# Order in a mixing stage's first and last steps: shared products ahead of bias products, page bookkeeping behind the norm, small loads split, two additions a tile

## What is computed

```python
attn_out = ctx @ o_w + o_b + xn
an = _rmsnorm(attn_out, gamma2)
shared = gelu(an @ sh_w1 + sh_b1) @ sh_w2 + sh_b2
logits = an @ router_w + router_b
aff = softmax(logits)
topv, topi = top_k(aff, 3)                       # 31 experts
gates = sum(one_hot(topi, 31) * topv)
routed = sum_e gates_e * (gelu(an @ re_w1_e + re_b1_e) @ re_w2_e) + gates @ re_b2
return shared + routed + an + attn_out           # plus the residual x
```

## Time and profile before

| | us |
|---|---|
| median of 3 runs | 1021.67 (1016.75 to 1024.92) |
| the profiled execution, its own time | 1016.59 |
| its span, first to last instruction | 1014.9 |
| mixing stage within it | about 700 to 849 |
| expert stage | 849 to 1015 |

### The profile page before, as it was taken

One profiled execution on the slowest core, in us unless ns is written; L12 is line 12 of the kernel. 1 busy time (PEld: TensorE's weight loads), 2 busy tenths in 40 slices (PEclk: granted clock), 3 DMA queues, 4 the chain that ended last, 5 costly groups with the idle time before them and its releaser, 6 DMA issues. The chain is left out here.

```text
span 1014.9 us, 18998 instructions
## 1 busy us (share of the span) xinstructions
PE 926.5 (91%) x5504; PEld 689.4 (68%) x5504; DVE 654.6 (64%) x1983; ACT 546.5 (54%) x1370; POOL 451.9 (45%) x584
## 2 busy tenths in 40 slices
PE   7979999996999999959999899999799789999997
PEld 4655555664766666747776676766678546999996
DVE  5966686782696979858777677772366632334555
ACT  5657888784342424447876677763122222555553
POOL 6013574544877887922123222250556440003652
PEclk9979999998999999969999999999899766999999
DMA  7657646433668677889778777763959421445775
GB/s 245 215 179 222 179 127 169 129 97 106 232 231 306 232 283 260 320 255 240 195 192 201 219 199 191 194 195 79 273 190 373 152 99 54 135 133 169 230 229 173
DMA packets 151702, 200.48 MB, mean 198 GB/s; under 512 B 21914, under 2 KB 94393, under 8 KB 151602
## 3 DMA queue, kind: packets, MB, share of 16 engines
q1 hardware_dynamic: 140674, 179.00, 58.1%
q0 software_dynamic: 4608, 12.59, 4.1%
q10 hardware_dynamic: 6320, 7.69, 2.6%
HBM read 121.37 MB, written 77.73 MB: 196 GB/s over the span
## 5 line engine op out<-in xcount | busy, mean ns | idle before, releaser
L1004 DVE CUSTOM_DVE_ANT_0 a_sm<-a_sc,keep_mask_qk 128x512 f32<-128x512 f32 (+3 forms) x256 | 118.4, 482 | 68.8 <-PE a_sc L918 59.9
L716 DVE CUSTOM_DVE_ANT_0 rope_x<-a_sc,keep_mask_qk 128x512 bf16<-128x512 f32 (+3 forms) x256 | 112.1, 486 | 51.3 <-PE a_sc L611 48.3
L992 ACT ACTIVATE a_probs<-a_sm,a_neg 128x512 f32<-128x512 f32 (+3 forms) x256 | 140.1, 552 | 4.0 <-DVE a_neg L1004 3.9
L1318 POOL TENSOR_TENSOR rope_rot<-rope_wqkv 128x512 f32<-128x512 f32 x64 | 93.2, 1473 | 30.8 <-DVE rope_wqkv L1384 30.5
L923 PE MATMUL a_tp<-keep_ident,a_probs 128*128 128x128 f32 x640 | 104.4, 280 | 0.0
L2029 POOL DMA_INDIRECT ex_three<-ks,keep_slots x48 | 48.2, 1005 | 118.7 <-SPq L2053 96.2
L923 PEld LDWEIGHTS a_tp<-keep_ident,a_probs 128*128 128x128 f32 x640 | 74.7, 141 | 25.6 <-issue 17.4
L897 POOL CAST a_ka<-a_ka 64x512 fp32r<-64x512 f32 x48 | 29.2, 609 | 130.8 <-DMA a_qa<-qs 130.2
L1256 PE MATMUL p_ub<-rope_km,rope_wh 128*128 128x512 f32 x256 | 82.0, 402 | 6.0 <-DVE rope_km L1374 6.0
L2139 DVE COPY ex_w<-keep_w 128x514 f32 x78 | 33.5, 430 | 81.7 <-ACT ex_hid L2101 79.3
L2078 PE MATMUL ex_hb<-ex_xT,ex_w 128*128 128x128 f32 x624 | 84.2, 279 | 0.7 <-DVE ex_xT L2141 0.7
(11 more groups left out here) (297 smaller groups left out, 2144.9 us busy)
## 6 DMA issues: line engine op xcount, KB each, us to landing
a_qa<-qs SPq DMA_DIRECT2D x96, 128.0 KB, 3.9
ks<-rope_rot SPq DMA_DIRECT2D x40, 256.0 KB, 3.3
qs<-rope_rot SPq DMA_DIRECT2D x40, 256.0 KB, 2.5
keep_ring<-qs SPq DMA_DIRECT2D x78, 128.0 KB, 2.5
ks<-ex_ysb SPq DMA_DIRECT2D x78, 128.0 KB, 2.2
rope_qm<-qs SPq DMA_DIRECT2D x64, 128.0 KB
rope_km<-ks SPq DMA_DIRECT2D x64, 128.0 KB
qs<-rope_qm SPq DMA_DIRECT2D x32, 256.0 KB, 2.6
```

The lines of the kernel that those rows point to most:

```text
L716: return dve.tensor_tensor_reduce(out=junk[:, JUNK[qb]:JUNK[qb] + n], in0=src, in1=c.mask_qk[:, S - n:S], scale=1.0, scalar=-3e38, op0=ALU ...
L992: act.activation(probs[:, h % PR, rows(qb)], sm[:, h % SM, rows(qb)], ACT.Exp, bias=neg[:, h % 2, qb:qb + 1], scale=-1.0, accum_out=sums[: ...
L1004: return dve.tensor_tensor_reduce(out=sm[:, h % SM, rows(qb)], in0=src[:, 0:n], in1=c.mask_qk[:, S - n:S], scale=-1.0, scalar=3e38, op0=AL ...
L1318: pool.tensor_tensor(rot[:, u % ROT, half, :], prod[:, u % 2, 2 * half, :], prod[:, u % 2, 2 * half + 1, :], op)\
```

## The change

It reorders and splits; only flags of accumulation and where some values stand in PSUM go with it.

1. Small loads: `ob` is issued first on a semaphore of its own (`ob_in`), for which alone POOL's first `bias` waits. `small_in` counts seven: `g2`, `sb2`, `rb`, `sb1`, `rw`, `sw1`, `sw2`. `x1` of step 0 and then `b2` (`b2_in`) are issued by ACT behind `pre(0)`. DVE's `base(0)` moves behind `norm(0)`.
2. `place` is cut in two. Its second half, `settle(b-1)`, stands behind `norm(b)` and ahead of `shared(b-1)`.
3. Behind `hidden(3, 1)` PE does the row product for the table of experts (now into `tp[1]`), then `shared(3)`, then the gates' turns and bias products; the last step's bias products (`last_bias`) come at the very end. `turn_gate` alternates between `tp[0]` and `tp[1]`. DVE copies the table ahead of its bias additions.
4. In `experts`, the additions of step 2 go two to a round, so 12 are left behind the loop instead of 14. Tiles 8 to 11 are stored in the loop; 12 and 13 by ACT and 14 and 15 by POOL at the end.

```diff
         shift_b, end_b, new_b = (tp[1][:, 256 + 32 * i:256 + 32 * i + E] for i in range(3))
-        row_b = tp[0]
+        row_b = tp[1]
         bias_bank = (op[0], op[1], hp[0], hp[1], op[0], op[1])
...
         tile_of, rowed, tables_known = (a.sem(n) for n in ("tile_of", "rowed", "tables_known"))
-        small_in, factors_in, last_scaled = (a.sem(n) for n in ("small_in", "factors_in", "last_scaled"))
+        small_in, ob_in, b2_in, factors_in, last_scaled = (a.sem(n) for n in ("small_in", "ob_in", "b2_in", "factors_in", "last_scaled"))
         x1_in = [a.sem(f"x1_in{i}") for i in range(B)]
...
         block = a.stack.enter_context(nc.Block())
-        NSMALL = 9
+        NSMALL = 7
         LAST = B * H // 2 - 4
...
         def _(act):
+            act.dma_start(ob[:, :], t["L0_ffn_o_b"].to_broadcast([P, D])).then_inc(ob_in, 16)
+            for dst, name in ((g2, "L0_ffn_gamma2"), (sb2, "L0_ffn_sh_b2"), (rb, "L0_ffn_router_b")):
+                act.dma_start(dst[:, :], t[name].to_broadcast([P, dst.shape[1]])).then_inc(small_in, 16)
+            act.dma_start(sb1[:, :], t["L0_ffn_sh_b1"]).then_inc(small_in, 16)
             for dst, name, pat in ((rw, "L0_ffn_router_w", "(k p) n -> p k n"),
...
                 act.dma_start(dst[:, :, :], t[name].rearrange(pat, p=P)).then_inc(small_in, 16)
-            for dst, name in ((ob, "L0_ffn_o_b"), (g2, "L0_ffn_gamma2"), (sb2, "L0_ffn_sh_b2"), (rb, "L0_ffn_router_b")):
-                act.dma_start(dst[:, :], t[name].to_broadcast([P, dst.shape[1]])).then_inc(small_in, 16)
-            act.dma_start(sb1[:, :], t["L0_ffn_sh_b1"]).then_inc(small_in, 16)
-            act.dma_start(b2[:, :], t["L0_ffn_re_b2"]).then_inc(small_in, 16)
...
+            pre(0)
             load_x1(0)
-            pre(0)
+            act.dma_start(b2[:, :], t["L0_ffn_re_b2"]).then_inc(b2_in, 16)
             for b in range(B - 1):
...
                     act.wait_ge(bias_mul, b - 1)
-                act.activation(gateT[:, b % 2, :], tp[0][0:E, :], ACT.Copy).then_inc(g_copied, 1)
+                act.activation(gateT[:, b % 2, :], tp[b % 2][0:E, :], ACT.Copy).then_inc(g_copied, 1)
             for j in range(2):
...
-            def shared(b, more=False):
+            def shared(b):
...
                             mm = pe.matmul(yp[j][:, D * (i % 2):D * (i % 2) + D], hid[:, m, P * i:P * i + P], sw2[:, m, :],
-                                           start=(m == 0), stop=(m == FF // P - 1 and not more))
-                        if more:
-                            mm = pe.matmul(yp[j][:, D * (i % 2):D * (i % 2) + D], gateT[:, b % 2, P * i:P * i + P], b2[:, :],
-                                           start=False, stop=True)
+                                           start=(m == 0 and i % 2 == 0), stop=(b < B - 1 and m == FF // P - 1 and i % 2 == 1))
+                    if b < B - 1:
+                        mm.then_inc(y_mul, 1)
+
+            def last_bias():
+
+                pe.wait_ge(g_copied, B)
+                for j in range(2):
+                    for i in (2 * j, 2 * j + 1):
+                        mm = pe.matmul(yp[j][:, D * (i % 2):D * (i % 2) + D], gateT[:, (B - 1) % 2, P * i:P * i + P], b2[:, :],
+                                       start=False, stop=(i % 2 == 1))
                     mm.then_inc(y_mul, 1)
...
-                if b:
-                    pe.wait_ge(g_copied, b)
+                if b >= 2:
+                    pe.wait_ge(g_copied, b - 1)
+                elif b == 1:
+                    pe.wait_ge(tables_known, 1)
                 for i in range(SB):
-                    mm = pe.transpose(tp[0][0:E, P * i:P * i + P], gate[:, SB * b + i, :], c.ident[:, :])
+                    mm = pe.transpose(tp[b % 2][0:E, P * i:P * i + P], gate[:, SB * b + i, :], c.ident[:, :])
                 mm.then_inc(g_turned, 1)
...
             hidden(B - 1, 1)
+            pe.wait_ge(tile_of, 1)
+            pe.wait_ge(place_read, B)
+            pe.matmul(row_b[0:1, 0:P], of_tile[:, :], c.ident[:, :], start=True, stop=True).then_inc(rowed, 1)
+            shared(B - 1)
+            pe.wait_ge(b2_in, 16)
             pe.wait_ge(gate_ready, 1)
...
             bias(2)
-            pe.wait_ge(g_copied, B)
-            shared(B - 1, more=True)
-            pe.wait_ge(tile_of, 1)
-            pe.matmul(row_b[0:1, 0:P], of_tile[:, :], c.ident[:, :], start=True, stop=True).then_inc(rowed, 1)
+            last_bias()
...
                 if b == 0:
-                    pool.wait_ge(small_in, 16 * NSMALL)
+                    pool.wait_ge(ob_in, 16)
                 pool.wait_ge(xn_in[b % 2], 16 * (b // 2 + 1))
...
                 dve.tensor_copy(c.slots[:, :, cols], pos[:, :, cols]).then_inc(slots_ready, 1)
+
+            def settle(b):
...
             for b in range(B):
-                base(b)
+                if b:
+                    base(b)
                 outputs(b)
...
                 if b:
+                    settle(b - 1)
                     shared(b - 1)
+                else:
+                    base(b)
                 more_base(b)
...
             place(B - 1)
+            settle(B - 1)
...
+            dve.wait_ge(rowed, 1)
+            dve.tensor_copy(c.experts[:, 0:NT], row_b[0:1, 0:NT]).then_inc(tables_known, 1)
             for b in range(B - 1):
...
                     dve.tensor_add(tiles, tiles, bias_bank[j][:, :]).then_inc(bias_added, 1)
-            dve.wait_ge(rowed, 1)
-            dve.tensor_copy(c.experts[:, 0:NT], row_b[0:1, 0:NT]).then_inc(tables_known, 1)
             dve.wait_ge(tick_s, gates_k)
...
             "turned", "x_copied", "w_copied", "h_mul", "h_done", "y_mul", "y_copied", "ye_done"))
-        tick_s, summed, out_s = a.sem("tick"), a.sem("summed"), a.sem("out")
+        tick_s, summed, out_s, out_p = (a.sem(n) for n in ("tick", "summed", "out", "out_p"))
         block = a.stack.enter_context(nc.Block())
...
             return TOPK * SB * (q // SB) + SB * k + q % SB + 1
+
+        added = [MOST[n // (TOPK * SB)] + 2 + (n % (TOPK * SB)) // (1 if n < 2 * TOPK * SB else 2) for n in range((B - 1) * TOPK * SB)]
+
+        def store_out(eng, q, done):
+            eng.wait_ge(summed, adds(q, TOPK - 1))
+            eng.dma_start(out[q // SB, P * (q % SB):P * (q % SB) + P, :], c.base[:, q, :]).then_inc(done, 16)
...
                             .then_inc(three_in[q % SUMS][k], 16)
-
-        def store_out(eng, q):
-            eng.wait_ge(summed, adds(q, TOPK - 1))
-            eng.dma_start(out[q // SB, P * (q % SB):P * (q % SB) + P, :], c.base[:, q, :]).then_inc(out_s, 16)
+            for q in range(TILES - 2, TILES):
+                store_out(pool, q, out_p)
...
                     sp.nop(nofuse=True).then_inc(ye_done, 1)
-                for b in range(B - 2):
-                    q = n - (MOST[b] + 2 + TOPK * SB)
-                    if SB * b <= q + SB * b < SB * b + SB:
-                        store_out(sp, q + SB * b)
-            for q in range(SB * (B - 2), SB * (B - 1)):
-                store_out(sp, q)
-            sp.wait_ge(out_s, 16 * TILES)
+                for b in range(B - 1):
+                    q = n - (added[TOPK * SB * (b + 1) - 1] + 1)
+                    if 0 <= q < SB:
+                        store_out(sp, SB * b + q, out_s)
+            sp.wait_ge(out_p, 16 * 2)
+            sp.wait_ge(out_s, 16 * (TILES - 2))
...
                     act.activation(ysb[:, n % YR, :], yb[n % 2][:, 0:D], ACT.Copy).then_inc(y_copied, 1)
-            for q in range(SB * (B - 1), TILES):
-                store_out(act, q)
+            for q in range(SB * (B - 1), TILES - 2):
+                store_out(act, q, out_s)
...
             ADDS = TOPK * TILES
-            first_round = {r: n for b in range(B - 1) for n in range(SB * TOPK * b, SB * TOPK * (b + 1))
-                           for r in [MOST[b] + 2 + n - SB * TOPK * b] if r < NT}
-
             dve.wait_ge(c.w1_in, 16 * c.w1_loads)
...
                     last_part(r)
-                if r in first_round:
-                    add(first_round[r])
-            for n in range(len(first_round), ADDS):
+                for n, round_ in enumerate(added):
+                    if round_ == r:
+                        add(n)
+            for n in range(len(added), ADDS):
                 add(n)
```

## The result

| | kernel before | kernel after |
|---|---|---|
| device time, median of 4 runs | 1021.71 us (1016.75 to 1024.92) | 1008.38 us (1005.39 to 1009.71) |
| ratio to before | 1 | 0.987 [0.982, 0.992] |
| profiled execution: time, span | 1016.59, 1014.9 us | 1009.71, 1007.8 us |

The change makes the kernel 13.3 us faster by the medians. Beside the first experiments the changed kernel ran once more, on another chip: 1009.06 against 1019.54 us, 0.9906 [0.9885, 0.9927].

The account below looks back on a forecast made before the run. PE, busy 91% of the span, was taken as the bound, with gains where it idles or runs slow. Front 4.7 + tail 13.5 + end 1.0 = 19.2 us; 997.4 from the profiled execution, 1002.5 from the median, taken 999.5, range 990 to 1010.

Parts of the forecast that it names:

- a clock that stays low through the tail: Rival, end of mixing stage: clock stays low, tail gains only 6.4 us, 1004.5 us in all; chance 0.14.
- the front: Start of the mixing stage: 3.9 + 3.1 − 2.3 = 4.7 us gained, bounds 0 and 7.
- The wait for small loads and the clock behind it: Mixing stage's front: PE restarts 3.9 us earlier, and the stretch at half speed behind it saves 3.1 us.
- `x1(0)` late: Front: x1(0), issued later, lands after 8.5 us and holds up DVE; 2.3 us given back, bounds 0 and 4.
- Pages settled: Step 3 of the mixing stage: bookkeeping behind the norm lets PE start 1.8 us earlier, counted inside the 13.5.
- The tail: End of mixing stage: shared products ahead of bias products start the expert stage 13.5 us earlier, bounds 6.4 and 14.9.
- Two additions a tile, and the stores: End of expert stage: additions 1.2 us earlier, last stores partly over POOL; 1.0 us gained, bounds −1 and 1.7.
- front wait changes its owner: Rival, front: small loads or x1 land later and the clock drops anyway; front gains 0, 1002.1 us, chance 0.14.

Follow-up runs that it names:

- Experiment 2: Changed kernel with the load of x1(0) issued ahead of the first norm again; 998.40 us, 0.9795 of the kernel before.
- experiment 7: Changed kernel with the page bookkeeping of steps 0 to 2 back ahead of the norm; 1008.51 us, 0.9881 of the kernel before.
- experiment 8: Changed kernel with the last two output tiles stored from ACT's queue, not GpSimd's; 1006.00 us, 0.9856 of the kernel before.
- both again (9): Changed kernel with x1(0) ahead of the first norm and the last stores from ACT, second run; 996.35 us, 0.9763 of the kernel before.
- GpSimd aside (10): Changed kernel, x1(0) first, last stores from ACT, GpSimd's factor products held until step 0's membership is written; second run 996.16 us, 0.9776.
- experiment 4: Kernel before with only load_x1(0) moved behind pre(0) and base(0) behind the norm; 1019.25 us, 1.0014 of the kernel before.
- experiment 6: Changed kernel with step 3's shared products back behind the bias products of steps 0 to 2; 1013.58 us, 0.9938 of the kernel before.
- experiments 5: Kernel before with the order of the last step alone changed as in the change; 1006.38 us, 0.9857 of the kernel before.

## Why the prediction was right, and where it was not

The whole time, 1008.4 us, lies inside the range of 990 to 1010 and 9 us above the forecast. That it lies inside is luck in part. The forecast's own range was 993 to 1004, and the time is outside it. The wide range reached 1010 for another rival, a clock that stays low through the tail; that did not happen, and the loss that did, in the front, fell outside its own bounds and happened to fit in. Term by term:

- **The wait for small loads and the clock behind it (3.9 + 3.1).** Right. Idle 1.44 us for the 1.7 foreseen, granted clock 1.00 behind it, 7.17 us for 32 products. Experiment 2 measures it free of the rest: 6.0 us for 7.0.
- **`x1(0)` late (−2.3).** This term failed. Two sizes were off and one thing was missing. The landing: 8.5 us assumed, 10.96 and 10.4 measured, at and just above my upper end (10.6). Those rows were the nearer ones for the size, but not the same case throughout: the load with 10.6, `x1(0)` of the kernel before (issued at 705.52, landed at 716.13), had no weights ahead of it, only the small loads and `xn`; the one with 10.2 did stand behind SP's weights. What it held up: the logit addition came 4.5 us after PE's products were through, where I had 2.3 (2.1 by the prediction's own times, 729.3 less 727.2). Missing: when PE idled again (6.27 us), the clock fell again. I had priced this fall as a gain where it vanished and at nothing where a new wait could bring it back. It costs 1.8 us in the first eight products alone. The term is −7.2 (front of after less front of experiment 2), outside my bounds of 0 to −4.
- **GpSimd beside DVE (no term).** The factors landed later too, since all that SP issues went out later, and so GpSimd's products, which before had begun at 728.20 and been over by 732.8, ran through DVE's choice. I had said of `xn(2)` and the next `x1` what their lateness does, and of the factors nothing. What this cost by itself no run separates.
- **Pages settled (1.8, in the tail).** The wait is as worked out: 3.87 us, released by DVE's `keep_bounds`, 1.74 us less. Its value in the stage is 1.1 us (experiment 7).
- **The tail (13.5).** Right in size (14.2) and in mechanism: L1649 directly behind L1764 at clock 1.00, PE's wait for the gates gone. I had reckoned with either PE or SP as what ends the stage, and taken SP. In the kernel after it is PE, whose clock falls at the second bias group; with PE fast it is SP. The two bounds lie within 1 us of each other, which is why the forecast was good in spite of the wrong owner. The rival of a low clock through the tail is out. (By the prediction's own terms its end at the high clock is 829.1 and not 828.9; nothing hangs on it.)
- **Two additions a tile, and the stores (1.0).** The additions: 1.4 us earlier, for 1.2. In the loop they are hidden, as foreseen: four of the six rounds with two additions take the 1.98 us of all others, and the remaining two make it up between them (2.33, then 1.63). The stores: −1.6 for −0.2. I had compared landings (3.1 for 2.1) and not asked what else ends an execution behind a store of GpSimd's queue. The sentence of the Trainium skill (DMA: Bandwidth & Descriptors, Latency and other measured facts) that puts the software path behind the hardware path in its first byte pointed the right way; the trace has 2.8 us to landing for GpSimd's two stores and 2.1 for ACT's, but experiment 8 shows about three times that difference, 2.0 us, at the end.
- **The sum.** 19.2 foreseen, 12.9 measured in the trace: front −1.2 for 4.7, tail 14.2 for 13.5, end −0.1 for 1.0. 1021.7 − 12.9 = 1008.8, the median is 1008.4. Of the 9 us by which the forecast missed, 6 come from the sum and 3 from my taking a value between the profiled execution and the median. The 5 us between those two look like scatter in other stages: this stage started at 695.3 to 705.7 in the traces of unchanged code above it. If so, nothing of it was the change's to win, and the median was the right base; there is only one trace of the kernel before to judge by.
- The rival "front wait changes its owner" (1002.1, chance 0.14) had the mechanism, with 4.7 as its largest loss. It was 5.9.

## What to carry to other kernels

Here a load that was moved behind a stage's opening loads took its place in the line behind what had been issued before it, on another queue too: price such a load from the loads that had the same ones ahead of them, and follow what is queued behind its reader until an engine with no slack is reached. When an idle stretch is removed and its clock penalty counted as a gain, the same penalty belongs in every term that may open a new gap. And where two engines end a stage within a microsecond of each other, gains on either side don't add: measure from a fixed instruction to a fixed instruction, part by part, before believing a sum.

## What the runs showed of the hardware

**DVE's small operations beside GpSimd's.** The same addition on 128x124 elements (the last `member` of step 0) took 0.29 us in all six traces in which GpSimd was idle at that moment, and 0.69 to 1.23 in all eight in which it multiplied or added in SBUF. Five of them:

| kernel | GpSimd during the choice | three comparisons | last `member` addition |
|---|---|---|---|
| before | adds until 738.35, the addition is at 738.86 | 2.22 us | 0.29 us |
| after | multiplies, adds | 3.12 | 0.69 |
| x1 first (2) | multiplies | 1.75 | 1.23 |
| both again (9) | idle until 731.78 | 0.68 | 0.29 |
| GpSimd aside (10) | idle | 0.68 | 0.29 |

DMA was much the same: over DVE's choice of step 0 the DMA share was 1.09 in experiment 2 and in 9, at 324 and 307 GB/s. PE and ACT showed nothing of it; PE's eight hidden products took 3.60 us in all of these kernels and each Gelu 0.69. GpSimd pays too: four additions took 3.75 us beside DVE's `base(0)` and 2.77 without it, and all the difference is in the one that starts inside `base(0)`, 1.71 us for 0.72. The Trainium skill (SBUF — State Buffer, SBUF: two separate sides) calls the port pair of VectorE and GpSimd an exclusive lock for a whole instruction, which takes in a VectorE operation with two SBUF inputs beside a GpSimd operation that reads SBUF. The trace agrees, and gives the price for operations this small: a factor of 2.4 to 4.6. The logit addition of the same size, with one input in PSUM, took 0.28 us in the kernel after with GpSimd multiplying beside it (737.20), which fits too. One thing the two inputs don't cover: the cast ahead of the comparisons (128x12, one input in SBUF) took 0.70 us in the kernel after and 0.17 in experiment 4, beside GpSimd both times; why, no row shows.

**The clock through the tail.** In experiment 6 PE did gate turns and bias products for 14.93 us without a gap, all at 0.50, and the clock rose in the shared products behind them. In the kernel after it was at 1.00 through the shared products and fell in the second bias group with PE busy throughout. In experiments 5 and 7, with the same order but the turn of step 3 1.7 us later, the same groups all ran at 1.00. What decides it, no run here shows.

**A store through GpSimd's queue at the very end** cost 2.0 us against ACT's queue, three to four times the difference in landing (2.8 us, for ACT's 2.1 in the same kernel and 2.3 in experiment 8). What the rest of it is, no row shows.
